# Second cross attention of a two-layer decoder: where in a turn the heads are weighed, and how PSUM's banks are shared out

## The reference

```python
qh = (q @ Wq).reshape(B, N, 16, 64).transpose(0, 2, 1, 3)      # q: layer norm of x
kh = (kv @ Wk).reshape(B, M, 16, 64).transpose(0, 2, 1, 3)     # kv: the context, M = 361
vh = (kv @ Wv).reshape(B, M, 16, 64).transpose(0, 2, 1, 3)
attn = softmax(einsum('bhnd,bhmd->bhnm', qh, kh) * 64 ** -0.5)
out = einsum('bhnm,bhmd->bhnd', attn, vh)
x = x + out.transpose(0, 2, 1, 3).reshape(B, N, 1024) @ Wo + bo
```

## Time and profile before

| | us |
|---|---|
| median of 3 runs | 3377.37 |
| lowest, highest | 3372.01, 3384.0 |
| profiled execution | 3402.53 |
| its span | 3400.7 |
| TensorE busy in the span | 3199.8 (94%) |
| VectorE busy | 1770.2 (52%) |
| ScalarE busy | 1513.7 (45%) |
| mean granted TensorE clock | 0.976 of 2.4 GHz |

### The profile page before, as it was taken

The page is one execution under the profiler, slowest core; times in us unless marked ns, Lnnn a source line. Parts: engine busy times, 40 slices in busy tenths (PEclk is TensorE's granted clock), DMA queues, the critical chain, the costliest instruction groups (busy, mean ns, idle before and its releaser), DMA issues. The chain is left out here.

```text
span 3400.7 us, 77834 instructions
## 1 busy us (share of the span) xinstructions
PE 3199.8 (94%) x26274; PEld 2361.9 (69%) x26275; DVE 1770.2 (52%) x4700; ACT 1513.7 (45%) x4278; POOL 869.1 (26%) x982
## 2 busy tenths in 40 slices
PE   8999999799999898999998989999999999988992
PEld 6777777466666566777776767777777777756882
DVE  4655555466666543222224654666666666653433
ACT  4555555355555311222222346666666666631220
POOL 1000000211111101333332110223223223235874
PEclk9999999899999899999999999999999999989996
DMA  8600000400000332111113000100000000114786
GB/s 269 176 0 0 0 0 0 144 13 11 11 13 11 101 91 79 30 30 32 29 22 92 0 3 8 35 27 22 16 12 13 14 12 13 46 50 122 205 230 149
DMA packets 136648, 181.30 MB, mean 53 GB/s; under 512 B 36397, under 2 KB 108842, under 8 KB 135549
## 3 DMA queue, kind: packets, MB, share of 16 engines
q1 hardware_dynamic: 84272, 133.96, 12.9%
q0 software_dynamic: 45760, 26.67, 4.8%
q10 hardware_dynamic: 6540, 19.66, 1.7%
HBM read 116.11 MB, written 103.61 MB: 65 GB/s over the span
## 5 line engine op out<-in xcount | busy, mean ns | idle before, releaser
L1309 DVE TENSOR_REDUCE e_nmx<-PS 128x1 f32<-128x361 f32 x416 | 221.5, 532 | 360.6 <-PE PS L1156 354.6
L931 POOL DMA_INDIRECT slot_rows<-r_row,r_rows_now x256 | 257.0, 1004 | 345.8 <-DVE e_p L1316 292.6
L1156 PE MATMUL PS<-e_cT,e_qT 128*128 128x361 f32 x832 | 334.2, 484 | 0.7 <-issue 0.6
L1775 DVE TENSOR_REDUCE b_nmx<-PS 100x2 f32<-100x722 f32 x256 | 225.0, 906 | 181.6 <-PE PS L1569 181.6
L2706 PE MATMUL PS<-c_wgu,c_tile_xT 128*128 x912 | 290.8, 462 | 7.1 <-issue 6.3
L1261 ACT ACTIVATE e_pT<-PS 121x384 f32<-121x384 f32 (+1 forms) x416 | 199.4, 480 | 210.1 <-PE PS L1163 206.3
L1163 PEld LDWEIGHTS PS<-ident,e_p 128*121 128x121 f32 x1248 | 199.1, 185 | 97.3 <-issue 1.8
L1266 ACT ACTIVATE e_p<-PS,e_nmx 128x361 f32<-128x361 f32 x416 | 232.9, 560 | 35.2 <-DVE e_nmx L1309 33.8
L2706 PEld LDWEIGHTS PS<-c_wgu,c_tile_xT 128*128 128x128 f32 x912 | 169.8, 191 | 83.9 <-issue 9.1
L1156 PEld LDWEIGHTS PS<-e_cT,e_qT 128*128 128x128 f32 x832 | 146.1, 191 | 115.8 <-issue 109.1
L2972 POOL DMA_INDIRECT sum<-f_y,f_y_token x128 | 199.6, 1560 | 69.4 <-issue 55.8
(11 more groups left out here) (347 smaller groups left out, 6529.8 us busy)
## 6 DMA issues: line engine op xcount, KB each, us to landing
f_w<-in_f_W SPq DMA_DIRECT2D x64, 384.0 KB
slot_rows<-a_empty SPq DMA_DIRECT2D x1, 21504.0 KB, 65.3
f_xg<-slot_rows SPq DMA_DIRECT2D x64, 336.0 KB
c_wgu<-in_c_GU ACTq DMA_DIRECT2D x8, 1408.0 KB, 6.7
sum<-X SPq DMA_DIRECT2D x2, 3200.0 KB, 57.7
f_sums<-sum SPq DMA_DIRECT2D x16, 384.0 KB
b_cT<-in_ctx_T SPq DMA_DIRECT2D x32, 181.5 KB, 2.3
e_cT<-in_ctx_T SPq DMA_DIRECT2D x32, 181.5 KB
```

The lines of the kernel that those rows point to most:

```text
L931: pool.indirect_dma_start(out=self.rows, in_=self.row[:, u, :], in_offset=None, out_offset=bass.IndirectOffsetOnAxis(ap=self.rows_now[:, u ...
L1156: sr.fill_done(pe.matmul(sr.at(f"s{m}", ROWS, CTX), qT[:, at:at + ROWS], cT[:, u, 0:CTX], start=True, stop=True), f"s{m}")
L1309: dve.tensor_reduce(nmx[:, m:m + 1], sr.at(f"s{m}", ROWS, CTX), AX.X, ALU.max, negate=True).then_inc(max_ready, 1)
L1775: sr.move_done(dve.tensor_reduce(nmx[:, g // PAR % 2, 2 * half:2 * half + 2, 16 * (1 - r)], sr.both(f"s{g}{half}", S, CTX), AX.X, ALU.max, ...
```

## The change

All sixteen heads of a sequence are weighed at one place: sequence 0 in slot 8, sequence 1 in slot 21, where before 8 heads each stood in slots 3, 9, 16 and 22. Within that slot the weighing stands behind the scores and ahead of the transposes, where it stood behind the transposes; it waits for the sequence's last group of turned probabilities. ScalarE copies both results in that slot, behind the exponential. Scores have two banks where they had three, weighed sums two where they had one; the numbers of the other banks shift by one, and `mr` keeps its two.

```diff
-    WEIGH_AT = {3: (0, 0), 9: (0, 1), 16: (1, 0), 22: (1, 1)}
+    WEIGH_AT = {8: 0, 21: 1}
...
-        sr = Banks(k, 0, 3).plan([f"s{m}" for m in range(SLOTS)])
-        tr = Banks(k, 3, 2).plan([f"p{m}" for m in range(SLOTS)])
-        ob = Banks(k, 5, 1).plan([f"o{u}{b}" for u in range(2) for b in range(2)])
+        sr = Banks(k, 0, 2).plan([f"s{m}" for m in range(SLOTS)])
+        tr = Banks(k, 2, 2).plan([f"p{m}" for m in range(SLOTS)])
+        ob = Banks(k, 4, 2).plan([f"o{u}{b}" for u in range(2) for b in range(2)])
...
-                    tr.wait_moved(pe, t, f"p{u * GROUPS + (6, 12)[b]}")
+                    tr.wait_moved(pe, t, f"p{u * GROUPS + GROUPS - 1}")
...
                         if at:
                             scores(*at)
+                        if this and n in WEIGH_AT:
+                            for b in range(2):
+                                weigh(WEIGH_AT[n], b, i)
                         at = ahead(n, TURNED, i, this, nxt)
                         if at:
                             turn_probs(*at)
-                        if this and n in WEIGH_AT:
-                            weigh(*WEIGH_AT[n], i)
...
                         if this and n in WEIGH_AT:
-                            move_out(*WEIGH_AT[n], i)
+                            for b in range(2):
+                                move_out(WEIGH_AT[n], b, i)
```

## The result

The changed kernel takes 3430.19 us (median of 3 runs, 3425.3 to 3434.42) against 3377.37: a ratio of 1.0148, interval [1.0124, 1.0171]. In a later session beside the kernel before on one chip it was 3424.64 against 3377.63, 1.0142 [1.0121, 1.0163]. Forecast was 3423, slower.

What follows compares the result with a forecast made beforehand. TensorE was taken to bound the stage, busy 635.94 of 639 us. Terms of -0.6, +1.6, +0.6, +0.3, +0.5 and +1.0 made +3.4 us a turn, 48 over fourteen turns, taken as +46 on 3377.37: 3423, range 3388 to 3452.

Steps and rivals of the forecast that it cites:

- Slot 18: Queries wait for ScalarE's copies of slot 17's queries, held up through VectorE's late maximum behind the ranking: +1.6 us a turn.
- The sign that it read beforehand: Slot 18's queries already start 0.03 us late in the kernel before, so the cover there is already used up.
- Slot 24: Output product y1 waits for VectorE's reads of the routing positions' bank, behind slot 23's maximum: +0.6 us a turn.
- Slot 9: Routing logits wait for ScalarE's copy of slot 8's transposed rows, 3.16 us against TensorE's 2.97: +0.3 with the restart.
- Slots 3 to 5: Slot 4's scores wait for slot 2's bank, free when its exponential's sum is read: 0.4 to 0.5 us a turn.
- Ends of the lumps: Two weighing lumps fewer a turn save TensorE 0.30 us each at their ends: -0.6 us a turn.
- The hold on ScalarE: A fixed hold of some 2 us before the oT copies in slots 9 and 16, uncovered by the change: +1.0 a turn.
- rival D: New gaps on TensorE could lower the granted clock; 2 in 100, no time of its own.
- First and last turn: First turn, without routing: -0.6, with 0 to 0.5 for slot 4; last, without queries: about 0 to +2, taken as 1.
- Carrying a profile's microseconds over to the median: Profiled execution goes from 3402.53 to 3449 us; at full clock the same +46 was added to the median 3377.37.
- Rival A: No VectorE or ScalarE work is late, only the lumps' -0.6 a turn is left: -10 us, 3367; 7 in 100.
- Its deciding point: Slot 18: faster only if slot 17's maximum starts less than about 0.2 us behind its scores.

Runs made afterwards that it cites:

- Experiment 1: The changed kernel with VectorE's ranking piece moved from slot 16 to slot 13: 3393.33 us, 1.0034.
- experiment 3: The kernel before with only the change's banks (two for scores, two for sums), weighings left in their four slots: 3378.28 us, 0.9995.
- Experiment 7: The changed kernel with the ranking piece at slot 13 and the normalising piece of slot 22 at slot 21: 3389.32 us, 1.0042.
- experiment 9: The kernel of experiment 8 with ranking at slot 18, the next piece at 20 and the routing norm's statistics at slot 1: 3373.51 us, 0.9987.
- experiment 8: The changed kernel with ranking at slot 17, later pieces at 19 and 21, norm's statistics at slot 4, routing's transposed rows at 7: 3382.52 us, 1.002.
- experiment 4: The kernel before with VectorE's ranking piece moved from slot 16 to slot 13: 3384.1 us, 1.0015.
- experiment 6: The changed kernel with three banks for scores and one for transposed probabilities: 3425.96 us, 1.0142.
- experiment 2: The changed kernel with slot 18's three transposes done five times over into the same bank: 3425.01 us, 1.0132.

## Why the prediction was right

The time (3430 measured, 3423 said) and the sum a turn (+3.2 against +3.4) came out, and the mechanism of the largest terms is shown. But two terms of the sum were wrong and made up for each other, +1.0 that wasn't there and +0.7 that wasn't counted. That the total fits within 7 us is luck in this part. The other terms were forecast at 2.4 us a turn and measured at 2.5.

- *Slot 18, 1.6 us:* measured 1.77, through the chain as described. Experiment 1 shows the cause. This is the largest step. The sign that it read beforehand, queries 0.03 us late, was weaker than it looked: in experiment 3 they stand 0.42 behind the transposes and don't wait, their bank's copies ending 0.08 us earlier (2327.24 and 2327.32). The 0.03 goes with the late copy of e_oT in the profile before (below), which experiment 3 doesn't have.
- *Slot 24, 0.6:* 0.61. Experiment 7 took it away by moving the piece named. (The maximum could move up 1.82, 2340.12 less 2338.30, and not 1.78; that changes nothing.)
- *Slot 9, 0.3:* 0.19 ahead of the logits, which is the difference of 3.16 and 2.97 that the prediction worked out, and 0.08 more for the logits themselves (0.75 us against 0.67 in experiment 9, where nothing waits). *Slots 3 to 5, 0.5:* 0.44, of which the bank is only the last link; the prediction put it on slot 2's exponential, the root is slot 0's statistics (experiments 8 and 9).
- *Ends of the lumps, -0.6:* -0.47 as the remainder of the account, -0.70 in experiment 9, where the routing's rows also moved; a gain in both.
- *The hold on ScalarE, +1.0:* wrong, 0. The step failed where it took two late copies for a property of the code. They start 0.81 and 0.83 us behind the weighing's end in the profile before. In experiments 3 and 4, whose ScalarE programs are the same there, they start 0.04 and 0.05 us behind it; slot 16 of experiment 3 (the weighing ends at 2324.25):

```profile
2321.97 2.28 PE L1177 MATMUL PS<-e_pT,e_v 121*64 121x100 f32 x48
2324.30 0.50 ACT L1271 ACTIVATE e_oT<-PS 128x400 f32<-128x400 f32 x1 [1.19 <-PE PS L1177]
```

In the changed kernel the two copies follow straight on the exponential's read:

```profile
2317.41 0.20 ACT L1267 ACTIVATION_READ_ACCUMULATOR e_p<-PS,e_nmx 128x1 f32 x1
2317.50 0.90 ACT L1272 ACTIVATE e_oT<-PS 128x400 f32<-128x400 f32 x2
```

- *The clock, rival D, given 2 in 100 and no time:* wrong, 0.7 a turn. The argument that a gap of 2 us in 66 is small was no argument: the drop costs what lies behind the gap. By the Trainium skill (TensorE: Matmul & The Clock Gate, A second HAM failure mode: psum-queue depth-cycling), a kernel whose groups of matmuls had short idle stretches between them often enough went back and forth between the two clock levels and lost throughput. The trace agrees that short idle stretches bring the clock down. But here it was a single one of 1.70 us a turn, and each drop behind it cost 1.70 us.
- *First and last turn:* the last turn came out 2.1 us longer on experiment 3, inside the 0 to 2 given but for a tenth. The first was put at -0.6 to -0.1; with the filling it is 3.3 us longer, most of it a low clock that no term had.
- *Carrying a profile's microseconds over to the median* gave the right median and the wrong profile: the profiled execution was to take 3449 and took 3430. The stage took 63.8 us a turn in the profile before, but 63.2 in experiment 3, whose median is the kernel before's. So the profile's own difference, 27.7, is half of the true one.

Rival A's floor, that the ends of the lumps are a gain, turned out true, but only with VectorE's pieces moved (experiment 9), not with the change as made. Its deciding point, a maximum of slot 17 that isn't held up, was met by experiments 1 and 9 and not by the change.

## What to carry to other kernels

On a saturated engine a long block is also the cover for side work on the others: before moving it, list for each place it leaves what the other engines do there and who waits for them, and move that work along with the block. Ask of each such place how much slack it has now; slot 18 had 0.08 us and was the one that broke. Read a turn's length in more than one profile before building a term on a gap that only one shows. And give a new gap on a saturated engine a price beyond its own length: here the clock made a gap of 1.70 us cost 2.4 on average.

## What the runs showed of the hardware

After 1.70 us without a matmul, TensorE went to the 1.2 GHz level (granted 0.50) behind 12 of 28 gaps in the two profiles of the changed kernel. It stayed there for 3.4 us each time, starting 0.5 to 1.5 us after the restart. After 1.41 us (experiment 6) it did so behind none of 14 gaps, after 0.39 us (experiment 2) behind none of 14. Idle stretches of 0.21 us in slot 4 and 0.55 in slot 24 of the changed kernel were followed by full clock. What decides in which turns the drop comes isn't shown.

The profiled execution of the kernel before had three things that no other profile here shows. The first is a gap inside the weighing of slot 3 once a turn, 2.78 us from start to start against 2.21 in experiment 3. The second is the two late copies. The third is a row of idle stretches in the last turn that no engine's late end explains. There one weighing took 8.15 us, and the clock fell behind the stretches:

```profile
3001.27 1.59 PE L1177 MATMUL PS<-e_pT,e_v 121*64 121x100 f32 x31
3003.15 0.33 PE L1177 MATMUL PS<-e_pT,e_v 121*64 121x100 f32 x2 [0.30 <-issue]
3006.02 0.39 PE L1177 MATMUL PS<-e_pT,e_v 121*64 121x100 f32 x4 [1.03 <-issue]
3007.47 0.60 PE L1177 MATMUL PS<-e_pT,e_v 121*64 121x100 f32 x4 [1.06 <-issue]
```

```profile
3007.00:3020.00 13.00, 9.32 (x31) 6.72 (x32) 2.63 (x8) 2.63 (x8) 5.55 (x6) 0.50 0.04 8
```

None of these stretches is longer than 1.1 us, less than the single one of 1.41 that left the clock up. So the length of the longest stretch alone doesn't tell whether the clock falls.

Against experiment 3's profile these make most of the 25.6 us between the two spans: thirteen steady turns 8.0, the last turn 12, and 5.7 behind the stage. What caused them isn't settled; an expectation above calls the first a fetch gap, but no row shows a fetch. The kernel before was profiled once only. The kernels of experiments 3 and 4, nearly the same, show none of the three, and that experiment 3 has the kernel before's median speaks against the code as the cause.
